# Masking the diagonal block of the first score pass with one 128-row product instead of two 64-row products

## The chip, the cores and the metric

The kernel runs on one core of one Trainium2 chip. The time is the device time of that core in microseconds (us), as a median of several runs; lower is better. A core has a matrix engine (TensorE, here PE) that multiplies a loaded block of weights (up to 128 rows by 128 columns) with a stream of columns and writes to PSUM, and VectorE (DVE), ScalarE (ACT) and GpSimd (POOL) for everything else. SyncE (SP) issues DMA transfers. The engines run side by side and wait for one another on semaphores. PE's records are of two kinds: PEld is the load of weights, PE the product. Their ends are modelled from the size of the product, so start-to-start steps say more than durations.

## The reference

Two layers run one after the other on x of shape (2, 512, 128), conditioned by one row of 128 per batch. The first is a gated recurrent layer and an MLP with ternary weights and quantised activations. The second is causal attention with 16 heads of 8 columns and an MLP. The change touches only the scores of that attention:

```python
qkv = (x @ Wqkv).reshape(b, t, 3, H, hd).transpose(2, 0, 3, 1, 4)
q, k, v = (qkv[0], qkv[1], qkv[2])
scores = jnp.einsum('bhqd,bhkd->bhqk', q, k) * hd ** (-0.5)
causal = jnp.tril(jnp.ones((t, t), bool))
scores = jnp.where(causal, scores, -jnp.inf)
attn = jax.nn.softmax(scores, axis=-1)
out = jnp.einsum('bhqk,bhkd->bhqd', attn, v)
```

## The kernel before

The first layer takes the first half of the time, up to about 140 us. Then queries and keys are computed in fp32 and split into three bf16 parts each; DMAs stack six pairs of parts (8 rows each, 48 rows in all) into the tiles `QS` and `KS`, so that one bf16 product with 48 contracted rows gives a score at nearly fp32 accuracy. Heads 0 to 7 lie in rows 0 to 63 of these tiles and heads 8 to 15 in rows 64 to 127: a product uses one half of the array's rows, the lower or the upper one (`half_rows`).

Attention runs over eight groups (two batches, four groups of four heads: two heads of each half). A group goes through two passes:

- First pass: for each tile of 128 queries the scores are computed with queries on PSUM's partitions (`score_item`, L1401 to L1403), and VectorE takes their row maxima (L1139). There are 12 items in a group (`S_ITEMS`). Items 0 to 3 have two heads each, for query tiles 0 (128 keys) and 1 (256 keys). Items 4 to 7 have one head each for query tile 2 (384 keys), and items 8 to 11 for query tile 3 (512 keys), with heads of the two halves in turn. Three PSUM banks hold items in rotation, so an item waits until the item three places earlier has been read. After the last item VectorE splits the maxima into three bf16 parts (L1149 to L1152), PE transposes them (L1413), VectorE copies them (L1160), and a DMA puts them as three more rows into `QS`.
- Second pass: the scores again, transposed and less their maxima, in `exp_slot` (L1437 with masks L1440 and L1443, always for a head of each half together). ScalarE takes the exponential (L707), PE multiplies by the values (L1457) and transposes the result (L1290), and VectorE divides (L1168, L1169).

The two passes of different groups are interleaved by an order that is written out by hand in the code: a loop of rounds, in which PE takes score item i of group n, and after certain items a slot of the second pass of group n-1 or n-2 (`E_OLD`, `E_NEW`), the values of group n-2 (`PV_AT`) or the transposes of group n-3. So after items 2, 3, 5, 6 and 10 whole-array work follows (L1413, L1290, L1457), and after the other items a half-array product. VectorE takes the items in the same order. PE's queue is in program order.

The mask of the diagonal block is added on PE. Of each score product the last 128 key columns are the block with the query tile's own tokens. A matrix of -1e30 above the diagonal is added to it by products of an identity with the mask, accumulated into the same PSUM columns as the scores. As each head uses only 64 rows of the array, there are two such products: the first 64 query rows (`pickLo` with `maskQlo`, 128 columns) and the last 64 (`pickHi` with `maskQhi`, 64 columns, since the first 64 keys are allowed to all of them). The constants lie in `k_b` (bf16), a cast (L856) of `k_f`, which one DMA loads (L336).

Of the kernel before, what the change touches and what calls it, by code (L numbers as in the profile page):

```python
# [31 lines left out]
P = 128  # L32
# [18 lines left out]
def _spans(*items):  # L51
    at, out = 0, {}
    for name, width in items:
        out[name] = (at, at + width)
        at += width
    return out, at
# [7 lines left out]
                  ("ba4", OUT6), ("bproj", D), ("b2", D))  # L64
CC, CC_N = _spans(("cT", B), ("g", 2), ("be", 2), ("b1", 4), ("bada", 4))
R1, R1_N = _spans(("bgate", 2 * D))
KC, KC_N = _spans(("ident", P), ("pickLo", P), ("pickHi", P), ("maskQlo", P), ("maskQhi", P // 2),
                  ("maskKlo", P // 2), ("maskKhi", P), ("count", 16))

W4_ROUND = (0, 1, 2, 5)  # L70
# [10 lines left out]
SROWS = HD * len(Q_PART)  # L81
# [55 lines left out]
def build(nc, x, cond_w, wa4, cond_rows, main_w, l1_w, bcast_rows, cols, rows1, consts, out):  # L137
    with ExitStack() as ctx:
# [5 lines left out]
        def bank(i, n=1):  # L144
            return ps[:, i * 512:(i + n) * 512]
# [112 lines left out]
        ident = k_f[:, slice(*KC["ident"])]  # L258
        ident_b = k_b[:, slice(*KC["ident"])]

        def k_of(name, rows):
            return k_b[rows, slice(*KC[name])]

        def half_rows(j, n=ROWS):

            first = j // 2 * ROWS
            return slice(first, first + n)

        def slot_head(g, j):
            return g * 2 + j % 2  # L270

        def tok(t, n=D):

            return slice(t * n, (t + 1) * n)
# [18 lines left out]
        def cs_of(k, i, j=1):  # L293


            return cs[:, k, i:i + j]
# [4 lines left out]
        def weights(name, c=None):  # L301

            a, z = (CW if name in CW else MW)[name]
            n = {"wa2": D, "wm2": D}.get(name, z - a)
            return (cwq if name in CW else mwq)[:, a + (c or 0) * n:a + (c or 0) * n + n]
# [901 lines left out]
        def _(pe):  # L1207
            T = nc.tensor
# [44 lines left out]
            for i, j in enumerate((0, 1, 3, 4)):  # L1253
                ins = T.matmul(bank(4)[:, 16 + B * i:16 + B * (i + 1)], lw[:, a + j * D:a + (j + 1) * D], scT[:, :],
                               start=True, stop=True)
# [6 lines left out]
            for b in range(B):  # L1262
                ins = T.matmul(bank(4)[:, b:b + 1], crow[:, a + b * P:a + (b + 1) * P], cs_of(4, 7),
                               start=True, stop=True)
# [4 lines left out]
            for b in range(B):  # L1269
                for a in range(0, OUT6, 512):  # L1270
                    z = min(a + 512, OUT6)
                    for c in range(OC):
                        ins = T.matmul(bank(2 * b + a // 512)[:, 0:z - a], cxq[:, c, b:b + 1].to_broadcast([P, P]),
                                       w4q[:, c, a:z], start=(c == 0), stop=(c == OC - 1))
# [4 lines left out]
            for i, j in enumerate((2, 5)):  # L1279
                for b in range(B):  # L1280
                    dst = bank(5)[:, (2 * i + b) * D:(2 * i + b + 1) * D]
                    T.matmul(dst, scT[:, b:b + 1].to_broadcast([P, P]), lw[:, a + j * D:a + (j + 1) * D],
                             start=True, stop=False)
                    ins = T.matmul(dst, ones[0:1, :], row1[:, g0 + i * D:g0 + (i + 1) * D], start=False, stop=True)
# [44 lines left out]
            for t in range(NT):  # L1329
                for b in range(B):  # L1330
# [5 lines left out]
                    for j in range(2):  # L1336
                        ins = T.matmul(bank(4 * b + 2 * (t % 2) + j), xq3[b][:, 1, tok(t)],
                                       weights("wm1")[:, j * MLP:(j + 1) * MLP], start=True, stop=True)
# [31 lines left out]
            for b in range(B):  # L1370
# [3 lines left out]
                for i in range(2):  # L1374
                    T.matmul(bank(4 * b + 2 + i), lw[:, a + i * D:a + (i + 1) * D], xmT[b][:, :],
                             start=True, stop=True).then_inc(S["qk_pe"], 1)
                for t in range(NT):
                    ins = T.matmul(bank(4 * b)[:, tok(t)], xmT[b][:, tok(t)], lw[:, a + 2 * D:a + 3 * D],
                                   start=True, stop=True)
                ins.then_inc(S["v_pe"], 1)  # L1380

            def score_item(n, i):

                b, g = divmod(n, NG)
                k = NUMBER[n, i]
                qt, h0, nh = S_ITEMS[i]
                w = (qt + 1) * P
                if k >= 3:
                    pe.wait_ge(S["s_used"], k - 2)
                if i == 0:  # L1390
                    pe.wait_ge(q_stacked[b], 32 * len(Q_PART))
                    pe.wait_ge(k_stacked[b], K_SP)
                    pe.wait_ge(k_stacked_gp[b], K_GP)
                    pe.wait_ge(S["part2"], 2 * B)
                    pe.wait_ge(S["v_ready"], B)
                    pe.wait_ge(S["v_ones"], b + 1)
                for j in range(nh):
                    h = slot_head(g, h0 + j)
                    dst = bank(S_BANKS[k % 3])[:, j * w:(j + 1) * w]
                    rows, r = half_rows(h0, SROWS), half_rows(h0)  # L1400
                    T.matmul(dst, QS[b][rows, h, tok(qt)], KS[b][rows, h, 0:w], start=True, stop=False)  # L1401
                    T.matmul(dst[:, w - P:w], k_of("pickLo", r), k_of("maskQlo", r), start=False, stop=False)  # L1402
                    ins = T.matmul(dst[:, w - P // 2:w], k_of("pickHi", r), k_of("maskQhi", r), start=False, stop=True)  # L1403
                ins.then_inc(S["s_pe"], 1)

            def maxima(n):
# [83 lines left out]
            def down(b, t, c, dst):  # L1490

                pe.wait_ge(S["gelu_ready"], 4 * b + c + 1)
                return T.matmul(dst, hid[b][:, c * L + t * P:c * L + (t + 1) * P], w2_g[:, b, c * D:(c + 1) * D],  # L1493
                                start=(c == 0), stop=(c == MLP // P - 1))
# [3 lines left out]
            for n in range(N_GROUPS + 3):  # L1498
                for i in range(len(S_ITEMS)):
                    if n < N_GROUPS:  # L1500
                        score_item(n, i)
                    if i == 2 and 1 <= n <= N_GROUPS:
                        maxima(n - 1)
                    if i in E_OLD and 2 <= n <= N_GROUPS + 1:
                        exp_slot(n - 2, E_OLD[i])
                    if i in E_NEW and 1 <= n <= N_GROUPS:
                        exp_slot(n - 1, E_NEW[i])
                    if i == 3 and n >= 3:
                        values_rows(n - 3)
                    if i in PV_AT and 2 <= n <= N_GROUPS + 1:  # L1510
                        values(n - 2, PV_AT[i])
                    if n == N_GROUPS and i == 7:
                        pe.wait_ge(S["s_used"], NUMBER[N_GROUPS - 1, "maxima"] + 1)
                        columns_of_attention(0)
                if n == N_GROUPS:
                    projection(0)
                if n == N_GROUPS + 1:
                    norm_columns(0)
# [6 lines left out]
            for t in range(NT):  # L1525
                for c in range(MLP // P):
                    ins = down(0, t, c, bank(W2_BANKS[0])[:, tok(t)])
# [3 lines left out]
            for c in range(MLP // P):  # L1531
                for t in range(NT):
                    ins = down(1, t, c, bank(W2_BANKS[1] + t)[:, 0:D])
# [66 lines left out]
```

## Time and profile before

| | |
|---|---|
| median of the runs | 289.58 us (289.57 to 290.57, 3 runs) |
| the profiled execution's own time | 289.72 us |
| its span, first to last instruction | 287.6 us |
| PE busy | 160.0 us, 56% |
| VectorE busy | 188.6 us, 66% |
| ScalarE busy | 139.1 us, 48% |
| L1401, 128 products | 36.5 us |
| L1402, 128 products | 27.2 us |
| L1403, 128 products | 23.9 us |
| mean granted clock | 0.798 |

Times inside the profile count from the first instruction. A busy time is the time in which at least one record of the engine or line is open. PE's records overlap, and each goes on for some time after its last column has entered, so PE's busy time is no sum of work. The granted clock is the share of TensorE's full clock that the chip grants: 1.00 is 2.4 GHz, 0.50 is 1.2 GHz. Idle time in brackets names what ended it.

### The profile page before, as it was taken

How to read it: one execution, taken by the hardware profiler on the slowest of the kernel's cores; microseconds unless marked ns; L12 is line 12 of the kernel's file. 1: busy time of each engine (PE TensorE's matmuls, PEld its weight loads, DVE VectorE, ACT ScalarE, POOL GpSimd, SP SyncE). 2: the span in 40 equal slices, each digit the busy share in tenths (PEclk: the TensorE clock that was granted, in tenths of full speed). 3: DMA queues.
4: the chain of work that ended last, by engine and by line, in shares of the span. 5: the costliest groups of instructions: out<-in, count | busy, mean ns of one | idle time of the engine just before them, and what ended most of it. 6: DMA issues, size and time to landing. Idle time of an engine off the chain costs nothing.

```text
span 287.6 us, 4182 instructions
## 1 busy us (share of the span) xinstructions
PE 160.0 (56%) x1493; PEld 102.1 (35%) x1495; DVE 188.6 (66%) x528; ACT 139.1 (48%) x297; POOL 69.5 (24%) x77
## 2 busy tenths in 40 slices
PE   0212239444733006227580009579999999897985
PEld 0102135243512003027350006254564456354664
DVE  0687797999966985965852009657897788715320
ACT  3455877557845036933164000045466446676621
POOL 7061621326035152960168000000000000003110
PEclk9999999857555556857777555559999999999999
DMA  6992000000000000000048555500000000000010
GB/s 190 417 396 125 1 0 0 0 2 1 0 0 1 0 0 0 1 2 0 0 72 89 69 69 72 70 4 4 4 3 1 5 4 2 4 2 3 0 39 36
DMA packets 5355, 12.15 MB, mean 42 GB/s; under 512 B 1075, under 2 KB 3604, under 8 KB 4692
## 3 DMA queue, kind: packets, MB, share of 16 engines
q1 hardware_dynamic: 4758, 11.09, 14.8%
q0 software_dynamic: 576, 0.79, 2.1%
q8 instruction: 12, 0.20, 0.3%
q14 instruction: 9, 0.07, 0.1%
HBM read 8.11 MB, written 0.52 MB: 30 GB/s over the span
## 4 chain that ended last, share of the span: by engine, by line
DVE 37%; PE 33%; DMA 10%; POOL 5%; SPq 5%; ACT 4%; issue 4%; DVEq 0%; ACTq 0%
DVE negmax L1139 9%; PE ps L1457 6%; DMA KS<-part 6%; PE ps L1290 5%; SPq L326 4%; PE ps L1401 4%; POOL uh L445 3%; DMA QS<-nmT 3%; PE ps L1487 2%; PE ps L1493 2%; DMA cw<-in_cond_w 2%; PE ps L1349 2%; PE ps L1437 2%; DVE xhat L810 2%; DVE u L967 2%
## 5 line engine op out<-in xcount | busy, mean ns | idle before, releaser
L1139 DVE TENSOR_REDUCE negmax<-ps 128x1 f32<-128x384 f32 (+3 forms) x96 | 52.6, 594 | 35.7 <-PE ps L1403 35.7
L707 ACT ACTIVATE PT<-ps 128x1024 f32<-128x1024 f32 x40 | 40.7, 1026 | 63.8 <-PE ps L1443 63.6
L1401 PE MATMUL ps<-KS,QS 48*128 48x384 bf16 (+3 forms) x128 | 36.5, 344 | 21.1 <-DMA KS<-part 20.8
L379 POOL TENSOR_TENSOR rstd<-veps,mhalf 128x4 f32<-128x4 f32 x8 | 8.1, 1016 | 139.9 <-DVE veps L804 139.9
L1290 PE MATMUL ps<-k_f,u 128*128 128x128 f32 x40 | 10.0, 426 | 34.4 <-ACT u L631 23.4
L1437 PE MATMUL ps<-QS,KS 51*128 51x512 bf16 (+3 forms) x128 | 24.6, 315 | 5.1 <-DMA QS<-nmT 5.0
L1402 PE MATMUL ps<-k_b 64*128 64x128 bf16 x128 | 27.2, 245 | 0.0
L1401 PEld LDWEIGHTS ps<-KS,QS 48*128 48x128 bf16 x128 | 11.7, 100 | 37.5 <-issue 22.5
L1403 PE MATMUL ps<-k_b 64*128 64x64 bf16 x128 | 23.9, 208 | 0.0
L1457 PE MATMUL ps<-PT,V 128*9 128x512 f32 (+3 forms) x256 | 22.5, 434 | 1.9 <-ACT PT L707 1.2
L1290 PEld LDWEIGHTS ps<-k_f,u 128*128 128x128 f32 x40 | 7.6, 221 | 36.2 <-DVE u L967 28.1
L1443 PE MATMUL ps<-k_b 64*128 64x128 bf16 x128 | 18.2, 222 | 0.0
L1440 PE MATMUL ps<-k_b 64*128 64x64 bf16 x128 | 17.5, 196 | 0.0
L1403 PEld LDWEIGHTS ps<-k_b 64*128 64x128 bf16 x128 | 13.2, 111 | 6.7 <-issue 2.4
L379 POOL TENSOR_TENSOR rms<-vms,mhalf 128x4 f32<-128x4 f32 x10 | 10.2, 1033 | 21.0 <-DVE vms L941 20.8
L1220 PE MATMUL ps<-k_f,cq 2*128 2x2 f32 x14 | 2.3, 249 | 19.0 <-DVE cq L830 19.0
L810 DVE TENSOR_SCALAR xhat<-xs,bnmv,rstd 128x128 f32<-128x128 f32 x32 | 10.8, 401 | 3.0 <-POOL rstd L379 2.9
L1402 PEld LDWEIGHTS ps<-k_b 64*128 64x128 bf16 x128 | 12.2, 104 | 0.0
L1437 PEld LDWEIGHTS ps<-QS,KS 51*128 51x128 bf16 x128 | 9.4, 96 | 7.1 <-DMA QS<-nmT 6.0
L1349 PE MATMUL ps<-k_f,uh 128*128 128x128 f32 x32 | 6.4, 386 | 9.7 <-DVE uh L1102 9.7
L445 POOL TENSOR_TENSOR uh<-prod,brow 128x512 f32<-128x512 f32 x8 | 9.8, 1270 | 5.2 <-DVE prod L1089 5.2
L1443 PEld LDWEIGHTS ps<-k_b 64*128 64x128 bf16 x128 | 9.2, 98 | 3.0 <-issue 0.6
(200 smaller groups left out, 435.0 us busy)
## 6 DMA issues: line engine op xcount, KB each, us to landing
w<-in_wa SPq DMA_DIRECT2D x2, 1152.0 KB, 10.7
QS<-part SPq DMA_DIRECT2D x24, 64.0 KB
brow<-in_bcast_rows SPq DMA_DIRECT2D x1, 1152.0 KB, 15.9
lw<-in_l_w SPq DMA_DIRECT2D x1, 1152.0 KB
mw<-in_main_w SPq DMA_DIRECT2D x1, 1024.0 KB, 13.5
KS<-part POOLq DMA_DIRECT2D x12, 64.0 KB, 5.6
KS<-part SPq DMA_DIRECT2D x12, 64.0 KB
cw<-in_cond_w SPq DMA_DIRECT2D x1, 576.0 KB, 5.9
```

The source lines that it names most:

```text
L379: return nc.gpsimd.tensor_tensor(r, v, mhalf[0:v.shape[0], 0:v.shape[-1]], ALU.pow)
L445: nc.gpsimd.tensor_tensor(uh[b][:, t, :], prod[b][t % 2][:, :], brow_of("nm2"), ALU.mult).then_inc(S["uh_raw"], 1)
L707: nc.scalar.activation(PT[n % 2][:, s, :], bank(2 * (use % 2), 2), ACT.Exp).then_inc(S["p_ready"], 1)
L1139: V.tensor_reduce(negmax[n % 2][:, qt, h0:h0 + nh], bank(S_BANKS[k % 3])[:, 0:nh * w].rearrange("p (h w) -> p h w", w=w), AX.X, ALU.max, n ...
L1290: ins = T.transpose(dst[:, tok(t)], src(t), ident)
L1401: T.matmul(dst, QS[b][rows, h, tok(qt)], KS[b][rows, h, 0:w], start=True, stop=False)
L1402: T.matmul(dst[:, w - P:w], k_of("pickLo", r), k_of("maskQlo", r), start=False, stop=False)
L1403: ins = T.matmul(dst[:, w - P // 2:w], k_of("pickHi", r), k_of("maskQhi", r), start=False, stop=True)
L1437: T.matmul(dsts[half], KS[b][rows, h, tok(kt)], QS[b][rows, h, kt * P:L], start=True, stop=False)
L1440: T.matmul(dsts[half][:, 0:P // 2], k_of("pickLo", r), k_of("maskKlo", r), start=False, stop=False)
L1443: ins = T.matmul(dsts[half][:, 0:P], k_of("pickHi", r), k_of("maskKhi", r), start=False, stop=True)
L1457: ins = T.matmul(bank(6)[32 * j:32 * j + HD + 1, kt * P:L], V1[b][:, kt, g * HG + j, :], src, start=(kt == 0), stop=(kt == 2))
```

## The change

Each score product gets one mask product instead of two. It takes the whole 128 by 128 identity as weights and the whole 128 by 128 mask as stream, over all 128 rows of the array, whichever half the head lies in. The constants lose two of their blocks (192 columns become 128). The second pass keeps its two masks.

```diff
-KC, KC_N = _spans(("ident", P), ("pickLo", P), ("pickHi", P), ("maskQlo", P), ("maskQhi", P // 2),
+KC, KC_N = _spans(("ident", P), ("pickLo", P), ("pickHi", P), ("maskQ", P),
                    ("maskKlo", P // 2), ("maskKhi", P), ("count", 16))
...
-                    rows, r = half_rows(h0, SROWS), half_rows(h0)
+                    rows = half_rows(h0, SROWS)
                     T.matmul(dst, QS[b][rows, h, tok(qt)], KS[b][rows, h, 0:w], start=True, stop=False)
-                    T.matmul(dst[:, w - P:w], k_of("pickLo", r), k_of("maskQlo", r), start=False, stop=False)
-                    ins = T.matmul(dst[:, w - P // 2:w], k_of("pickHi", r), k_of("maskQhi", r), start=False, stop=True)
+                    ins = T.matmul(dst[:, w - P:w], ident_b, k_of("maskQ", slice(0, P)), start=False, stop=True)
...
-        "consts": _np.concatenate([eye, eye[lo], eye[hi], mask_q[lo], mask_q[hi][:, P // 2:], mask_k[lo][:, :P // 2],
+        "consts": _np.concatenate([eye, eye[lo], eye[hi], mask_q, mask_k[lo][:, :P // 2],
```

On PE this is the place around items 8 and 9 of a round. A row is the line, the operation, what it writes and reads, and the shape of its output; L1457 is the values, L1401 the score product, L1402 and L1403 its masks, L1437 to L1443 a slot of the second pass. Before:

```order
L1457 MATMUL ps<-PT,V 9x128 x4
L1401 MATMUL ps<-KS,QS 128x512
L1402 MATMUL ps<-k_b 128x128
L1403 MATMUL ps<-k_b 128x64
L1401 MATMUL ps<-KS,QS 128x512
L1402 MATMUL ps<-k_b 128x128
L1403 MATMUL ps<-k_b 128x64
L1437 MATMUL ps<-QS,KS 128x512 x2
```

After, at the same place (lines behind L1402 have moved up by one):

```order
L1456 MATMUL ps<-PT,V 9x128 x4
L1401 MATMUL ps<-KS,QS 128x512
L1402 MATMUL ps<-k_b 128x128
L1401 MATMUL ps<-KS,QS 128x512
L1402 MATMUL ps<-k_b 128x128
L1436 MATMUL ps<-QS,KS 128x512 x2
```

One row of each score product is gone, 128 in all, and nothing has changed its place; L1402 now reads all 128 rows. On VectorE only the cast at L856 has another width (720 instead of 784 columns), on SyncE only the load of the constants.

## Rows read from the trace of the kernel before

**Rows 1.** The page, busy time of the engines over the whole span

```profile
PE 160.0 (56%) x1493; PEld 102.1 (35%) x1495; DVE 188.6 (66%) x528; ACT 139.1 (48%) x297; POOL 69.5 (24%) x77
```

**Rows 2.** Stretches: busy us (count) of PE, PEld, DVE, ACT, POOL, PEclk, DMA share, GB/s

```profile
172.18:181.50 9.32, 9.01 (x75) 5.76 (x77) 8.46 (x20) 0.00 (x0) 0.00 (x0) 0.50 0.58 72
...
187.00:188.00 1.00, 0.00 (x0) 0.00 (x0) 0.00 (x0) 0.00 (x0) 0.00 (x0) 0.50 0.13 17
188.85:194.86 6.01, 5.96 (x71) 4.25 (x72) 4.43 (x11) 4.07 (x4) 0.00 (x0) 0.50 0.01 1
...
199.59:248.28 48.69, 45.21 (x682) 25.28 (x680) 39.33 (x96) 27.38 (x31) 0.00 (x0) 1.00 0.01 3
```

**Rows 3.** Timeline of VectorE: start us, us, operation, count, [idle before <-releaser]

```profile
216.90 0.56 DVE L1139 TENSOR_REDUCE negmax<-ps 128x1 f32<-128x384 f32 x1 [0.65 <-PE ps L1403]
...
219.06 0.69 DVE L1139 TENSOR_REDUCE negmax<-ps 128x1 f32<-128x512 f32 x1 [0.49 <-PE ps L1403]
```

**Rows 4.** Timeline of PE, the stretch that PE leads

```profile
215.47 1.04 PE L1457 MATMUL ps<-PT,V 128*9 128x512 f32 x8
216.45 0.33 PE L1401 MATMUL ps<-KS,QS 48*128 48x384 bf16 x1
216.62 0.22 PE L1402 MATMUL ps<-k_b 64*128 64x128 bf16 x1
216.68 0.19 PE L1403 MATMUL ps<-k_b 64*128 64x64 bf16 x1
216.80 0.83 PE L1457 MATMUL ps<-PT,V 128*9 128x384 f32 x8
217.56 0.33 PE L1401 MATMUL ps<-KS,QS 48*128 48x384 bf16 x1
217.57 0.39 PE L1437 MATMUL ps<-QS,KS 51*128 51x512 bf16 x1
```

**Rows 5.** Timeline of PE around the transposes of L1413 and L1290

```profile
213.04 0.39 PE L1413 MATMUL ps<-k_b,nmpart 128*12 128x128 bf16 x4 [0.61 <-DVE negmax L1139]
213.37 0.28 PE L1401 MATMUL ps<-KS,QS 48*128 48x256 bf16 x1
...
213.75 0.19 PE L1403 MATMUL ps<-k_b 64*128 64x64 bf16 x1
213.87 0.66 PE L1290 MATMUL ps<-k_f,pvs 128*128 128x128 f32 x4
214.46 0.33 PE L1401 MATMUL ps<-KS,QS 48*128 48x384 bf16 x1
```

**Rows 6.** Timeline of PE, whole-array and one-row products in one accumulation

```profile
50.38 0.48 PE L1284 MATMUL ps<-row,ones 1*128 1x128 f32 x2
50.79 0.49 PE L1282 MATMUL ps<-lw,scT 128*128 128x128 f32 x2
```

**Rows 7.** Timeline of PE's weight loads at the place of rows 4

```profile
216.46 0.10 PEld L1402 LDWEIGHTS ps<-k_b 64*128 64x128 bf16 x1
...
216.79 0.12 PEld L1457 LDWEIGHTS ps<-PT,V 128*9 128x9 f32 x8
```

**Rows 8.** Timeline of PE at the lower clock, up to the restart

```profile
180.54 0.59 PE L1413 MATMUL ps<-k_b,nmpart 128*12 128x128 bf16 x4 [0.25 <-DVE negmax L1139]
181.06 0.39 PE L1401 MATMUL ps<-KS,QS 48*128 48x256 bf16 x1
...
188.90 0.61 PE L1437 MATMUL ps<-QS,KS 51*128 51x512 bf16 x2 [5.01 <-DMA QS<-nmT]
```

**Rows 9.** Timeline of PE at score items 8 and 9

```profile
218.56 0.40 PE L1401 MATMUL ps<-KS,QS 48*128 48x512 bf16 x2
...
218.87 0.39 PE L1437 MATMUL ps<-QS,KS 51*128 51x512 bf16 x2
...
219.18 0.38 PE L1401 MATMUL ps<-KS,QS 48*128 48x512 bf16 x1
```

**Rows 10.** Timeline of VectorE, the first wait after the cast of the constants

```profile
10.40 0.16 DVE L766 TENSOR_TENSOR wraw<-ps,k_f 128x2 f32<-128x2 f32 x1 [1.72 <-PE ps L1214]
```

## The prediction

> **What bounds the kernel now.** First the page: no engine is full over the span, PE 56%, VectorE (DVE) 66%, ScalarE (ACT) 48% [rows 1]. The change touches only the attention stage, so these shares decide nothing. Next the table by stretches [rows 2]: the 48.69 us from 199.59 to 248.28 are five equal rounds of 9.74 us at a granted clock of 1.00, each with the 12 score items of one group of four heads. Divided by five, a PE record is open for 9.04 us of a round (records overlap, so PE's work is less), VectorE works for 7.87 us and ScalarE for 5.48. Who waits for whom tells more. In the round that ends at 219.06, VectorE [rows 3] waits for PE ahead of three of the larger items, the first time 0.65 us up to 216.90, the last time 0.49 us up to 219.06. PE waits for VectorE too, 0.61 us before the transposes of L1413 [rows 5]. The round is a chain that changes sides: PE leads from 215.47 [rows 4] to 219.06, some 3.6 us, VectorE most of the rest. Neither has much room.
>
> **What is removed and added.** Per score product (16 in a round, 128 in all) L1402 and L1403 go. L1403 starts 0.06 us after L1402 (216.62, 216.68 [rows 4]) and streams 64 columns, half of that, 0.03 us: together 0.09 us. The new product has 128 rows and 128 columns in bf16. The nearest row is L1413 [rows 5]: four records open for 0.39 us, one of them 0.22 (L1402's length, the same 128 columns), so a step of 0.17 / 3 = 0.056 us. By steps alone the change saves 0.03 us a product, 0.5 us a round.
>
> **The price that the diff doesn't show.** L1401 uses 48 rows of one half of the array, the new product all 128. Before, PE passes between half-array and whole-array work six times each way in a round. Read what a passage costs:
> - half to whole: L1403 starts at 216.68, its stream ends at 216.71, L1457 starts at 216.80: 0.09 us [rows 4]. The same from 213.75 to 213.87 ahead of L1290 [rows 5].
> - whole to half: the last L1413 starts at 213.21, streams to 213.26, and L1401 starts at 213.37: 0.10 us [rows 5].
> - in one accumulation: L1282 (128 rows) and L1284 (1 row) alternate in pairs into the same tile [rows 6], 0.41 us from pair to pair. Records of L1290, of the same 128 fp32 columns, take (214.46 - 213.87 - 0.10) / 4 = 0.12 us each [rows 5]; a pair so carries 0.17 us beyond two of them.
> - the weight load of a first product after a passage starts with the product, not ahead of it: L1457's at 216.79, while L1402's, within one half, starts 0.16 us before its product [rows 4, 7].
>
> So each mask costs 0.09 in, 0.056 for itself and 0.10 out, 0.25 us instead of 0.09. Eleven of 16 are enclosed by half-array work and pay both ways. Five (after items 2, 3, 5, 6 and 10) are followed by whole-array work and add only the way in before themselves; the one behind was paid before.
>
> No row shows this passage with bf16 on both sides and 128 weight columns. The bounds are 0 (the product joins like one more of the half's) and 0.14 us (at the lower clock: the last L1413 starts at 180.82, streams 0.11 us, L1401 starts at 181.06 [rows 8]). I take 0.09 and 0.10, since every passage that I read, fp32 or bf16, with 9, 12 or 128 weight columns, has about that.
>
> The Trainium skill, TensorEngine Tiling (Array Packing), Key Properties, says that a change of tiling mode drains the engine. It gives no time, and the sum doesn't use it.
>
> **What is lost beside it.** Items 8 and 9 lie in different halves and run side by side: both L1401 of 512 columns are in one 0.40 us row [rows 9]. So do L1401 and L1437 at 217.56 and 217.57 [rows 4]. A whole-array mask between them puts them one behind the other.
>
> **PE's work in one round of the changed kernel**, from start-to-start steps at full clock:
> - 16 score products, the step from L1401 to L1402 is 0.17 us for 384 columns [rows 4] and, by 0.053 per 128 columns, 0.06, 0.12 and 0.22 for 128, 256 and 512; four of each: 2.28
> - 16 masks of 0.056: 0.90
> - second pass (L1437, L1440, L1443), both halves side by side: 0.31 us for 512 columns (218.87 to 219.18 [rows 9]), so 0.09 beyond the columns' step; 0.31 + 0.26 + 0.21 + 0.15, twice: 1.86
> - values (L1457), from start to the next half-array product 0.98 for 512 columns and 0.76 for 384 [rows 4], so 0.22 per 128 columns, 0.54 and 0.32 for the other two; less four passages: 2.24
> - L1413 0.22, and L1290 0.49 (213.87 to 214.46 [rows 5], less a passage): 0.71
> - 17 passages in (16 masks, and L1457 after item 7's second pass) at 0.09, 17 out at 0.10: 3.2
>
> Together 11.2 us; a mask and an L1457 behind it are different whole-array forms, which may cost up to 0.09 three times. I take 11.3 us. That is over 9.74, so PE has no wait left and sets the time. The about 1 us that PE now waits hides the first part of the growth; VectorE's 7.87 and ScalarE's 5.48 us fit inside.
>
> **The sum.** Five rounds: 5 x (11.3 - 9.74) = +7.8. From the restart at 188.90 to 199.59 the clock is 0.50 until 194.86 [rows 2, 8]; a stream of 128 columns takes 0.107 us there and a passage about 0.13: 12 products at 0.37 instead of 0.18, 4 at +0.16, two pairs that no longer overlap, less PE's waits: +2.5 (1.6 to 4). Before that PE is already the slow side (9.01 of 9.32 us busy [rows 2]); 22 products at +0.19 move the copy of the first maxima by 4.2 us. But PE then waits 5.01 us for the DMA of these maxima [rows 8], and until about 187 the DMA engines still move what was issued earlier (from 187 to 188 they are 0.13 busy, and idle after the restart [rows 2]). So most is covered; the rest of group 1's items stays, +1.0 (0 to 2). After the last round three more items: +0.5. Behind the attention stage nothing changes. Sum +11.8 us on the profiled execution's own 289.72 us (span 287.6): 301.5. The median of the runs shown, 289.58, is 0.14 lower; I keep 301.5.
>
> The constants shrink from 784 to 720 columns. Their cast gets 64 of 784 columns shorter, and VectorE's next step waits 1.72 us for PE [rows 10]. Whatever of the cast is saved, a few hundredths of a us, is swallowed by that wait, and would be the whole gain without it.
>
> **Rivals.**
> - *The passage is free*, because the identity is loaded ahead and only both halves have to be done. Then a product saves 0.03 us, and the lost overlaps cost about as much in the 3.6 us that PE leads: 289 to 290 us, not slower. For it speaks that both operands are bf16 and that 8,192 fewer columns stream; against it the weight loads of [rows 7]. It decides below about 0.015 us a passage.
> - The Trainium skill, TensorE: Matmul & The Clock Gate, Part 2, step 1, would give this case: a weight load for the background buffer is pulled ahead of running products.
> - *Half the price*, 0.045 a way, since the whole-array product here is short: 34 x 0.05 less per round, so 9.6 to 10.4 us and 291 to 296.
> - *The clock stays down.* It is 0.50 while single halves work (172 to 181 us) and rises at 194.86, after 6 us in which both halves mostly work side by side [rows 2]. The change takes away much of that overlap. Each us by which the rise is late costs about 0.4 us. Should it not rise in the rounds, the 8.0 us of streams double: some 50 us more, about 350.
>
> **How the numbers follow.** Full price, the clock up within 7 us of its present place: 0.66, 297 to 308, likeliest 301.5. Half price 0.11, free 0.11, clock lost or much later 0.12. The range of 291 to 311 leaves out the free case and most of the lost clock. A measurement of this kernel tells about 0.5%, 1.4 us, from no change; the free case lies mostly inside that, with a third of it faster. Faster 0.04, same 0.08, slower 0.88.
>
> **What would show it.** 0.09 us between the end of L1401's stream and the mask, 0.10 between mask and next L1401; the mask's weight load starting with it; the L1401 of items 8 and 9 about 0.45 us apart; rounds of 11.3 us with PE never waiting; the wait of 5.01 us shrunk to below 2. It is wrong if the mask starts 0.01 to 0.02 us after L1401's stream: then the rounds are about 9.7 us and the time doesn't change.

## The result, and the profile after

The changed kernel is slower: ratio 1.0508 to the kernel before, interval [1.0453, 1.0563], which on 289.57 us is 304.3 us. The median of its four runs is 312.59 us, because two took 303.95 and 304.85 us at a mean granted clock of 0.797 and two 320.32 and 321.44 us at 0.743; the ratio is made from the first two, and why the others had less clock is open. The profiled execution took 303.95 us, its span 301.9 (before 289.72 and 287.6). The prediction was 301.5 us, 291 to 311.

The page of the changed kernel has, for the busy times of [rows 1] and then the chain of work that ended last:

```profile
PE 185.7 (62%) x1365; PEld 102.4 (34%) x1367; DVE 193.0 (64%) x528; ACT 139.9 (46%) x297; POOL 69.6 (23%) x77
...
PE 49%; DVE 26%; DMA 7%; POOL 5%; SPq 4%; ACT 4%; issue 3%; DVEq 0%; ACTq 0%
```

PE is busy for 25.7 us more with 128 fewer products. PE now carries 49% of the chain and VectorE 26%; before it was the other way round, 33% and 37%.

The table by stretches, with the columns of [rows 2]. The stretches are: from the first group's items to the restart with the second pass, the restart up to the clock's rise, the rest of that round, one round, five rounds:

```profile
172.00:186.60 14.60, 14.60 (x52) 5.17 (x51) 11.25 (x23) 0.00 (x0) 0.00 (x0) 0.50 0.47 62
186.60:200.50 13.90, 13.90 (x89) 5.31 (x88) 7.75 (x17) 5.12 (x5) 0.00 (x0) 0.50 0.00 1
200.50:203.60 3.10, 3.10 (x33) 1.11 (x29) 1.12 (x3) 0.73 (x1) 0.00 (x0) 1.00 0.02 5
203.60:215.30 11.70, 11.70 (x121) 5.30 (x120) 8.31 (x19) 5.62 (x7) 0.00 (x0) 1.00 0.01 2
203.60:262.11 58.51, 58.51 (x601) 26.52 (x600) 41.56 (x95) 28.04 (x31) 0.00 (x0) 1.00 0.01 2
```

The last row answers to the last one of [rows 2]: five rounds take 58.51 us instead of 48.69, so 11.70 each instead of 9.74, and PE is busy in every moment of them. Before, it was 45.21 of 48.69. VectorE has the same instructions (a record of it is open for 8.3 us a round, 7.9 before) and waits for the rest. The first row shows that the wait of 5.01 us [rows 8] is gone: PE works through.

Rounds are cut where VectorE starts the maxima of item 8 (L1139). These starts are at 176.82, 190.29, 199.59 us and then every 9.74 up to 248.28 before; after, at 177.43, 188.14, 203.60 and then every 11.70 up to 262.11. The span's +14.35 us so falls apart into four pieces:

| piece | before | after | difference |
|---|---|---|---|
| start to item 8 of group 1 | 190.29 | 188.14 | -2.15 |
| item 8 of group 1 to item 8 of group 2 | 9.30 | 15.46 | +6.16 |
| five rounds | 48.69 | 58.51 | +9.82 |
| item 8 of the last group to the end | 39.29 | 39.81 | +0.52 |

The timeline of PE in the changed kernel, at the place that answers to [rows 4 and 9] (L1456 is now the values, L1436 the second pass):

```profile
222.91 0.23 PE L1402 MATMUL ps<-k_b 128*128 128x128 bf16 x1
223.07 1.05 PE L1456 MATMUL ps<-PT,V 128*9 128x512 f32 x8
...
226.41 0.39 PE L1401 MATMUL ps<-KS,QS 48*128 48x512 bf16 x1
226.73 0.23 PE L1402 MATMUL ps<-k_b 128*128 128x128 bf16 x1
226.90 0.39 PE L1401 MATMUL ps<-KS,QS 48*128 48x512 bf16 x1
227.22 0.23 PE L1402 MATMUL ps<-k_b 128*128 128x128 bf16 x1
227.38 0.39 PE L1436 MATMUL ps<-QS,KS 51*128 51x512 bf16 x2
```

From L1401 to its mask it is 0.32 us. Four times 0.053 of that is the stream of 512 columns, 0.11 the passage into whole-array work. From the mask to the next L1401 it is 0.17, 0.056 stream and 0.11 the way out. Items 8 and 9, which were one row of two before [rows 9], now start 0.49 us apart. The weight loads at the same place:

```profile
226.41 0.09 PEld L1401 LDWEIGHTS ps<-KS,QS 48*128 48x128 bf16 x1 [0.22 <-DVE negmax L1139]
226.73 0.10 PEld L1402 LDWEIGHTS ps<-k_b 128*128 128x128 bf16 x1 [0.23 <-issue]
226.89 0.09 PEld L1401 LDWEIGHTS ps<-KS,QS 48*128 48x128 bf16 x1
```

The mask's weights load at 226.73, with their product and 0.32 us after the load before. The load's queue was idle for the 0.23 us ahead of it, and the profile puts this idle time down to nothing that it shows ("issue").

VectorE's side is seen in its timeline at items 6 and 8, which answer to the two rows of [rows 3] (0.65 and 0.49 us of waiting there), and in the waits of the five rounds (engine, line, waited for: us in total, times, longest):

```profile
224.59 0.56 DVE L1139 TENSOR_REDUCE negmax<-ps 128x1 f32<-128x384 f32 x1 [0.84 <-PE ps L1402]
...
227.00 0.69 DVE L1139 TENSOR_REDUCE negmax<-ps 128x1 f32<-128x512 f32 x1 [0.67 <-PE ps L1402]
```

```profile
ACT PT L707 <- PE ps L1442: 33.8, 26, 3.4
DVE negmax L1139 <- PE ps L1402: 15.5, 25, 0.8
```

The same view of the kernel before (199.59 to 248.28 us) has 23.3 us and 9.0 us there, and a wait of PE for VectorE that the changed kernel no longer has:

```profile
ACT PT L707 <- PE ps L1443: 23.3, 16, 2.0
DVE negmax L1139 <- PE ps L1403: 9.0, 16, 0.7
PE ps L1413 <- DVE negmax L1139: 3.0, 5, 0.6
```

### The profile page after: what moved, and what is told of

Read it like the earlier page. It is cut to its first block, busy times and chain, and to the rows that moved or that the text cites. A ratio compares the mean times of both kernels' runs of the same rounds, so it can differ in the third digit from the quotient of the medians.

```text
span 301.9 us, 3926 instructions
## 1 busy us (share of the span) xinstructions
PE 185.7 (62%) x1365; PEld 102.4 (34%) x1367; DVE 193.0 (64%) x528; ACT 139.9 (46%) x297; POOL 69.6 (23%) x77
## 4 chain that ended last, share of the span: by engine, by line
PE 49%; DVE 26%; DMA 7%; POOL 5%; SPq 4%; ACT 4%; issue 3%; DVEq 0%; ACTq 0%
PE ps L1401 11%; PE ps L1402 8%; PE ps L1456 7%; DMA KS<-part 5%; PE ps L1290 4%; PE ps L1436 4%; SPq L326 4%; POOL uh L445 3%; PE ps L1486 2%; PE ps L1492 2%; DMA cw<-in_cond_w 2%; PE ps L1349 2%; DVE xhat L810 2%; DVE u L967 2%; PE ps L1442 1%
## 5 line engine op out<-in xcount | busy, mean ns | idle before, releaser
L1139 DVE TENSOR_REDUCE negmax<-ps 128x1 f32<-128x384 f32 (+3 forms) x96 | 56.4, 600 | 46.8 <-PE ps L1402 45.3
L1401 PE MATMUL ps<-KS,QS 48*128 48x128 bf16 (+3 forms) x128 | 44.6, 348 | 19.6 <-DMA KS<-part 19.6
L1402 PE MATMUL ps<-k_b 128*128 128x128 bf16 x128 | 31.8, 249 | 0.0
L1290 PE MATMUL ps<-k_f,u 128*128 128x128 f32 x40 | 10.0, 426 | 34.6 <-ACT u L631 23.4
L1401 PEld LDWEIGHTS ps<-KS,QS 48*128 48x128 bf16 x128 | 12.4, 97 | 41.3 <-issue 22.7
L1456 PE MATMUL ps<-PT,V 128*9 128x512 f32 (+3 forms) x256 | 23.3, 447 | 1.5 <-ACT PT L707 1.2
L1402 PEld LDWEIGHTS ps<-k_b 128*128 128x128 bf16 x128 | 12.6, 98 | 25.1 <-issue 20.4
L1290 PEld LDWEIGHTS ps<-k_f,u 128*128 128x128 f32 x40 | 7.6, 220 | 36.4 <-DVE u L967 28.1
L1436 PE MATMUL ps<-QS,KS 51*128 51x512 bf16 (+3 forms) x128 | 19.0, 321 | 0.0
L1442 PE MATMUL ps<-k_b 64*128 64x128 bf16 x128 | 13.3, 223 | 0.0
L1439 PE MATMUL ps<-k_b 64*128 64x64 bf16 x128 | 12.2, 199 | 0.0
L586 ACT ACTIVATE junk<-mx 128x128 f32<-128x128 f32 x16 | 4.7, 297 | 11.3 <-DVE mx L936 11.3
L1349 PEld LDWEIGHTS ps<-k_f,uh 128*128 128x128 f32 x32 | 5.8, 206 | 10.0 <-DVE uh L1102 10.0
L1492 PEld LDWEIGHTS ps<-w_g,PT 128*128 128x128 f32 x64 | 7.8, 191 | 2.6 <-issue 1.4
```

The lines of the kernel that those rows point to most:

```text
L1139: V.tensor_reduce(negmax[n % 2][:, qt, h0:h0 + nh], bank(S_BANKS[k % 3])[:, 0:nh * w].rearrange("p (h w) -> p h w", w=w), AX.X, ALU.max, n ...
L1290: ins = T.transpose(dst[:, tok(t)], src(t), ident)
L1349: ins = T.transpose(bank(4 * b + c)[:, tok(t)], uh[b][:, t, tok(c)], ident)
L1402: ins = T.matmul(dst[:, w - P:w], ident_b, k_of("maskQ", slice(0, P)), start=False, stop=True)
L1436: T.matmul(dsts[half], KS[b][rows, h, tok(kt)], QS[b][rows, h, kt * P:L], start=True, stop=False)
L1442: ins = T.matmul(dsts[half][:, 0:P], k_of("pickHi", r), k_of("maskKhi", r), start=False, stop=True)
```

## The experiments

The kernel before had medians of 288.48 to 288.83 us on the chips of these runs. The length of a round is that of the rounds at full clock; "first round" is the one from item 8 of group 1 to item 8 of group 2, in which the clock rises. A visit is a stay in whole-array work, with a passage in and a passage out.

### The mask as two whole-array products

```diff
-ins = T.matmul(dst[:, w - P:w], ident_b, k_of("maskQ", slice(0, P)), start=False, stop=True)
+mask = k_of("maskQ", slice(0, P))
+T.matmul(dst[:, w - P:w - P // 2], ident_b, mask[:, 0:P // 2], start=False, stop=False)
+ins = T.matmul(dst[:, w - P // 2:w], ident_b, mask[:, P // 2:P], start=False, stop=True)
```

> The changed kernel, but each whole-array mask product is issued as two of 64 columns, one right behind the other. Passages between half-array and whole-array work: 17 each way in a round as before. If the price is that of the passage (measured in the changed kernel: 0.10 us in, 0.105 out), the second product only adds what a 64-column step costs more than its columns, 0 to 0.03 us: rounds of 11.7 to 12.2 us against 11.70, 304 to 308 us. If every whole-array product costs about 0.25 us because of its size or its weights, wherever it stands, the round grows by 16 x 0.25 = 4 us and the kernel takes about 335 us.

Ratio 1.0627 [1.0524, 1.0730]; the interval overlaps that of the changed kernel, so the totals don't tell the two apart and the rounds have to. A round takes 11.77 us, 0.07 more than with one product and not the 4 us more of the rival. The timeline of PE in this kernel:

```profile
215.45 0.39 PE L1401 MATMUL ps<-KS,QS 48*128 48x512 bf16 x1
215.77 0.20 PE L1403 MATMUL ps<-k_b 128*128 128x64 bf16 x1
215.81 0.19 PE L1404 MATMUL ps<-k_b 128*128 128x64 bf16 x1
215.94 0.39 PE L1438 MATMUL ps<-QS,KS 51*128 51x512 bf16 x2
```

The second half of the mask starts 0.04 us after the first; only the way in (0.32 from L1401, as before) and the way out (0.13, 0.10 beyond a stream of 0.03) carry the price. It belongs to the change of form, not to the product.

### One mask for two heads

Items 0 to 3 take both scores first and then one product of 256 mask columns (the mask read twice) for both. The edit, cut down to the products themselves:

```diff
-T.matmul(dst, QS[b][rows, h, tok(qt)], KS[b][rows, h, 0:w], start=True, stop=False)
-ins = T.matmul(dst[:, w - P:w], ident_b, k_of("maskQ", slice(0, P)), start=False, stop=True)
+T.matmul(dst, QS[b][rows, h, tok(qt)], KS[b][rows, h, 0:w], start=j == 0, stop=False)
+# behind the loop over the item's heads:
+T.matmul(bank(...)[:, 0:nh * w].rearrange("p (h w) -> p h w", w=w)[:, :, w - P:w], ident_b,
+         k_of("maskQ", slice(0, P)).unsqueeze(1).to_broadcast([P, nh, P]), start=False, stop=True)
```

> The changed kernel, but items 0 to 3, which have two heads in one bank, take both score products first and then one mask product over both diagonal blocks (256 columns, the mask read twice). The columns streamed are the same; passages fall from 17 to 13 each way. Passage theory: 4 x 0.2 us less in a round, 10.9 instead of 11.70 us, and about 1 us less in each of the two groups at the lower clock: 297 to 299 us. If the columns or rows of the mask set the price: no change, 304 us.

Ratio 1.0395 [1.0299, 1.0491], round 10.85 us: 0.85 less than 11.70 for four visits to whole-array work and back fewer, so 0.21 us each.

### The same, and items 8 and 9 with both scores ahead of both masks

```diff
-if n < N_GROUPS:
+if n < N_GROUPS and i == 8:
+    score_item(n, 8, (0,))
+    score_item(n, 9, (0,))
+    score_item(n, 8, (1,))
+    score_item(n, 9, (1,))
+elif n < N_GROUPS and i != 9:
     score_item(n, i)
```

`(0,)` calls for the scores of an item alone and `(1,)` for its mask.

> As the kernel with paired masks, and in addition items 8 and 9 issue both score products (one in each half, so side by side) and then both masks: 12 passages each way, and the overlap of these two comes back. Passage theory with lost overlap: 0.2 us for the passage and about 0.25 us for the overlap less, rounds of about 10.4 us, 293 to 296 us. If overlap is worth nothing: 10.7 us and 296 to 298. If neither counts: as the kernel with paired masks.

Ratio 1.0295 [1.0194, 1.0395], round 10.43 us. The timeline of PE has items 8 and 9 together again, and both masks in one row:

```profile
211.01 0.39 PE L1401 MATMUL ps<-KS,QS 48*128 48x512 bf16 x2
211.33 0.28 PE L1403 MATMUL ps<-k_b 128*128 128x128 bf16 x2
211.55 0.39 PE L1438 MATMUL ps<-QS,KS 51*128 51x512 bf16 x2
```

What started in 0.97 us before the second pass (226.41 to 227.38 of the changed kernel) starts in 0.54. The difference of 0.43 is that of the rounds, 10.85 to 10.43. It is one stream of 512 columns (0.21) and two passages (0.21). With five of the sixteen visits for a mask gone, the kernel is still 3% slower than before.

### The masks' columns alone: the kernel before without its second mask

This kernel leaves L1403 out, so that the last 64 queries of each diagonal block are unmasked in the first pass.

```diff
-T.matmul(dst[:, w - P:w], k_of("pickLo", r), k_of("maskQlo", r), start=False, stop=False)
-ins = T.matmul(dst[:, w - P // 2:w], k_of("pickHi", r), k_of("maskQhi", r), start=False, stop=True)
+ins = T.matmul(dst[:, w - P:w], k_of("pickLo", r), k_of("maskQlo", r), start=False, stop=True)
```

> The kernel before with its second mask product (L1403) left out: the last 64 rows of each diagonal block stay unmasked. One mask product instead of two, as in the change, but without a passage. If the product itself is worth what its step says (0.03 us on three or four products in the part of a round that PE leads), 288.5 to 289.6 us. If fewer products in the first pass free VectorE-led parts too, below 288. If it takes more than 290, the loss of the changed kernel has a cause beside the passages.

Ratio 1.0027 [0.9950, 1.0104], no difference beyond the noise; round 9.65 instead of 9.74. (Its first round took 10.59 us, with the clock low up to 196.8 us.) This is all that one mask product less could bring if it cost no passage: 0.09 us a round for 16 products whose work is 0.03 us each. The rest of their 0.5 us has to lie where PE would wait anyway.

### Meant to take the overlap alone away: the heads of one half behind one another

The kernel before, with the heads of items 4 to 11 in the order 0, 1, 2, 3 instead of 0, 2, 1, 3, so that items 8 and 9 use the same half.

```diff
-... for j in (0, 2, 1, 3)]
+... for j in (0, 1, 2, 3)]
```

> The kernel before with another order of heads: items 4 to 7 and 8 to 11 take the heads of the lower half first and then those of the upper, instead of in turn, so items 8 and 9 lie in the same half and can't run side by side. No mask is changed and no passage added. This is the lost overlap by itself. By the trace of before the pair is worth about 0.3 us in the part of a round that PE leads: rounds of 9.9 to 10.0 us instead of 9.74 and 290.5 to 292 us. If VectorE's pace hides it: 289 to 290.

Ratio 1.0045 [0.9997, 1.0094]: at most a small loss. The table by stretches, the first round and the five behind it:

```profile
188.90:200.14 11.24, 11.24 (x126) 6.26 (x124) 7.72 (x17) 5.20 (x6) 0.00 (x0) 0.62 0.01 3
200.14:248.83 48.69, 45.66 (x682) 25.81 (x680) 39.34 (x95) 27.53 (x31) 0.00 (x0) 1.00 0.01 3
```

The rounds at full clock are what they were, 9.74 us; the expectation for them was missed. The timeline of PE shows why:

```profile
219.42 0.38 PE L1401 MATMUL ps<-KS,QS 48*128 48x512 bf16 x1
219.43 0.39 PE L1437 MATMUL ps<-QS,KS 51*128 51x512 bf16 x1
219.64 0.22 PE L1402 MATMUL ps<-k_b 64*128 64x128 bf16 x1
```

The overlap is not lost but moved: item 9 now starts together with the second pass behind it, so from item 8 to the values behind item 10 it is 1.06 instead of 1.01 us. So this run doesn't show what an overlap is worth. Only the first round, mostly at half the clock, is longer, 11.24 instead of 9.30 us; its clock rose at 197.5 us, 2.4 us later than in the kernel before, so the order of heads need not be the reason.

### The clock raised ahead, in the changed kernel and in the kernel before

88 independent products of 384 columns ahead of the first score item and 30 (in the kernel before 36) ahead of the first slot of the second pass, into a bank that is free then.

```diff
+def fill(count):
+    for _ in range(count):
+        T.matmul(bank(6)[:, 0:3 * P], ident_b, k_b[:, 0:3 * P], start=True, stop=True)
```

> The changed kernel with filling products (whole-array, 384 columns, into a bank that is free) while PE waits for the stacked keys before the first score item (88 of them) and 30 more before the first second-pass slot. Theory that the late rise of the granted clock costs the rest of the loss and makes the time differ from run to run: the clock is 1.00 from the first score item on, the round from item 8 of group 1 to that of group 2 falls from 15.5 to about 11.5 us, 297 to 301 us, with runs close together. If the clock falls back between, or if the stretch is bound by something else: no change, 304, or more by what the filling delays.

> The kernel before with the same filling (88 products before the first score item, 36 in the 5 us wait for the first maxima's DMA). Before, the clock rises 6 us after the restart. If that costs as much as in the changed kernel, about 0.4 us for each us at the lower clock: 2 us less, 286 to 288. If the round at the lower clock (9.3 us) is bound by VectorE: no change, 288.5 to 290.

The changed kernel with it: ratio 1.0726 [1.0686, 1.0766], slower than without. The table by stretches, before and behind the clock's first fall, and the five rounds:

```profile
170.50:175.07 4.57, 4.57 (x25) 2.26 (x25) 3.31 (x7) 0.00 (x0) 0.00 (x0) 1.00 0.57 75
175.07:188.73 13.66, 13.66 (x48) 5.32 (x48) 8.75 (x19) 0.00 (x0) 0.00 (x0) 0.50 0.30 41
...
207.39:265.90 58.51, 58.51 (x601) 26.52 (x600) 41.57 (x96) 28.06 (x31) 0.00 (x0) 1.00 0.01 2
```

The clock was at 1.00 when the score items began, and fell at 175.07 though PE never waited. It was up again at 188.73, but fell once more at 195.55 and came back only at 205.79. The second block of filling was too long as well: it held PE up to 191.76, while the first exponential stands at 187.5 without it. So this run does not tell what an early clock would be worth: of its expectation the other branch came, the clock fell back and the filling delayed the rest. It does show that in this kernel a high clock at the start did not last, and that a round at full clock is 11.70 us with or without.

The kernel before with it: ratio 1.0118 [1.0082, 1.0154], so slower by 1.2%, and its median of 290.92 us lies above both expected ranges. Here too the second filling was too long: PE came to the second pass at 189.57 us, 18.5 us after the first maxima instead of 16.0. The clock fell at 175.31, rose at 185.55 and stayed. The first round then lies wholly at full clock:

```profile
190.38:199.48 9.10, 8.15 (x126) 4.56 (x124) 7.42 (x18) 5.38 (x6) 0.00 (x0) 1.00 0.02 4
```

It takes 9.10 us instead of 9.30. In the kernel before, 4.8 us of low clock so cost 0.2 us: at full clock PE has gaps in this round (8.15 of 9.10 us busy), and at the low clock it uses them up (9.30 of 9.30).

### Fewer passages in the kernel before: the values in two pairs

The kernel before with its own masks. The values, four blocks of eight L1457, come in pairs after items 5 and 10 instead of one by one after items 5, 6, 7 and 10.

```diff
-PV_AT = {5: 0, 6: 1, 7: 3, 10: 2}
+PV_AT = {5: (0, 1), 10: (3, 2)}
...
-    values(n - 2, PV_AT[i])
+    for kt in PV_AT[i]:
+        values(n - 2, kt)
```

> The kernel before with two passages less in a round and nothing else: the four blocks of values (L1457) are issued as two pairs, after items 5 and 10, instead of one after each of items 5, 6, 7 and 10. Same products, same columns. Passage theory: 0.19 us for each pair of passages in the part of the round that PE leads, rounds of 9.35 to 9.5 us instead of 9.74, 287 to 288.5 us. If passages cost nothing here, or VectorE leads that part once PE is faster: no change, 289.5; if the later items 6 and 7 starve VectorE: 290 to 292.

Ratio 0.9924 [0.9882, 0.9965], median 285.0 us: faster by 0.8%, and more than was expected. A round takes 9.19 us. The timeline of PE:

```profile
212.95 1.69 PE L1457 MATMUL ps<-PT,V 128*9 128x512 f32 x16
214.57 0.34 PE L1401 MATMUL ps<-KS,QS 48*128 48x384 bf16 x2
```

Sixteen products of the values in one visit, and behind them items 6 and 7 side by side, which the values had kept apart [rows 4]. At 0.2 us each, two visits fewer are 0.4 us of the 0.55, in the stretch that PE leads; the rest may be the two items side by side, which no run tells apart.

### That, and the transposes of L1290 moved next to those of L1413

```diff
+if i == 2 and n >= 3:
+    values_rows(n - 3)
...
-if i == 3 and n >= 3:
-    values_rows(n - 3)
```

> As the kernel with the values in two pairs, and the transposes of L1290 moved from behind item 3 to right behind the transposes of L1413 (item 2), so that one more pair of passages goes. This one lies in the part of a round that VectorE leads. If a passage is only worth something where PE leads: rounds of 9.2 us as before or up to 0.3 us longer, because item 3 now comes 0.3 us later: 285 to 287 us. If each pair of passages is worth 0.19 us wherever it is: 9.0 us and 284.

Ratio 0.9951 [0.9912, 0.9990], round 9.60 us, 0.4 more than without the move and more than either branch had expected. The timelines of PE and VectorE:

```profile
208.93 0.39 PE L1413 MATMUL ps<-k_b,nmpart 128*12 128x128 bf16 x4 [0.61 <-DVE negmax L1139]
209.25 0.65 PE L1290 MATMUL ps<-k_f,pvs 128*128 128x128 f32 x4
209.84 0.28 PE L1401 MATMUL ps<-KS,QS 48*128 48x256 bf16 x1
...
210.44 0.69 DVE L1139 TENSOR_REDUCE negmax<-ps 128x2 f32<-128x512 f32 x1 [0.32 <-PE ps L1403]
```

One passage more is saved, but item 3 comes 0.6 us later to VectorE, which sets the pace at this place (PE waits 0.61 us for it at L1413), and VectorE now waits 0.32 us for it. The delay outweighs the passage. What the passage would be worth here without a delay isn't shown.

### One mask for two heads, 8 and 9 together, and the values in pairs

The third experiment with the edit of `PV_AT` above.

> The kernel with whole-array masks, paired over items 0 to 3 and over items 8 and 9 (rounds of 10.43 us), and the values in two pairs after items 5 and 10. There the order of masks and values matters otherwise: items 6 and 7 now stand between half-array work and pay a way out that the values took over before, so the two passages saved by pairing the values come back at items 6 and 7. Passage theory: 12 passages each way as before, PE sets the pace, so no gain: rounds of 10.3 to 10.5 us, 295 to 297 us. If grouping the values is worth 0.5 us in a round by itself, as in the kernel with half-array masks (9.74 to 9.20): 9.9 us and 292.

Ratio 1.0143 [1.0081, 1.0204], round 10.09 us, 0.34 less than 10.43. The expectation of next to nothing was missed: it took a block of values behind a mask to share the mask's visit for free. The timeline of PE shows that it doesn't:

```profile
215.88 0.28 PE L1403 MATMUL ps<-k_b 128*128 128x256 bf16 x1
216.00 0.60 PE L1290 MATMUL ps<-k_f,pvs 128*128 128x128 f32 x4
...
217.62 0.23 PE L1403 MATMUL ps<-k_b 128*128 128x128 bf16 x1
217.78 1.69 PE L1458 MATMUL ps<-PT,V 128*9 128x512 f32 x16
```

From 256 mask columns to L1290, which also loads 128 weight columns, it is 0.12 us, little more than the stream of 0.107. From 128 mask columns to the values, which load 9 weight columns, it is 0.16, 0.10 beyond the stream. So the pairs save one passage after item 6 and two after item 7, 0.3 us.

## Why the prediction was right

Direction and size came out (+11.8 us forecast on the profiled execution, +14.2 measured, the median's ratio gives +14.7). Step by step:

**The price of a passage: right.** 0.09 and 0.10 were read from other forms; over the 16 masks of a round (215.19 to 226.90 us) the steps from L1401 to L1402 sum to 3.78 us, 2.13 of it streams, so 0.103 a way in. The steps from mask to half-array work are 0.162 us, 0.106 beyond the stream. The rival of a free passage falls with that (it wanted the mask 0.01 to 0.02 us behind the stream), the rival of half the price too. That the price is per change of form, not per product, was argued from rows and is shown by the split mask (0.07 us a round more instead of the 4 us that a price per product would have given).

**The weight load starts with the mask's product: right.** It was at 226.73 us, 0.32 us after the load before. The Trainium skill, TensorE: Matmul & The Clock Gate, Part 2, step 1, says that a load for the background buffer is pulled ahead of running products; between these forms it wasn't. The Trainium skill, TensorEngine Tiling (Array Packing), Key Properties, says that a change of tiling mode drains the engine, and the runs agree that such a change costs time, 0.10 us. How much of the 0.10 us is a drain and how much is a weight load that is no longer hidden, no run separates.

**PE never waits, rounds of 11.3 us: the mechanism right, one term too small.** The rounds are 11.70. The same sums, over the round above: L1401 to its mask 3.78 (forecast 3.72), mask to half-array work 1.78 (1.72), second pass 1.94 (1.95), values 2.63 (2.64, of which the forecast took the ways out off at 0.09 and put them back at 0.10, 0.04 us too much), L1412 and L1290 0.86 (0.91), and mask to whole-array work, five times, 0.70 (0.28 and the 0.1 allowed). The term that failed is the last, "a mask and an L1457 behind it are different whole-array forms, which may cost up to 0.09 three times": it is due in full, at 0.10, at the three blocks of values, and before the transposes of L1412 too, where 12 weight columns follow 128. So 9 or 12 weight columns act as another form than 128. The timeline of PE in the changed kernel has both kinds:

```profile
220.15 0.23 PE L1402 MATMUL ps<-k_b 128*128 128x128 bf16 x1
220.31 0.39 PE L1412 MATMUL ps<-k_b,nmpart 128*12 128x128 bf16 x4
...
221.22 0.23 PE L1402 MATMUL ps<-k_b 128*128 128x128 bf16 x1
221.28 0.61 PE L1290 MATMUL ps<-k_f,pvs 128*128 128x128 f32 x4
```

0.16 us from the mask to 12 weight columns, 0.06, its stream alone, to 128. The other way round it is the same: in the kernel with the transposes moved together, L1290 starts 0.32 us after L1413, 0.22 of it streams. Four times 0.10 instead of the 0.1 taken makes 0.3 of the missing 0.4 us, and passages of 0.105 instead of 0.09 and 0.10 most of the rest. Over five rounds that is 2.0 us, +9.8 instead of +7.8. Two experiments bear out the price: 4 visits fewer are 0.85 us, 3 passages fewer 0.34.

**The lost overlap: right in the changed kernel, where it stands in the sum.** Items 8 and 9 were to start about 0.45 us apart, and start 0.49 apart. With them together the round is 0.43 shorter, half of it the overlap. What the loss would be worth in the kernel before stays open, since the run meant for it only moved the overlap.

**From the restart to the round of group 2: too small, +6.2 instead of +2.5.** The first round, before and after:

```profile
190.29:199.59 9.30, 9.30 (x126) 5.71 (x124) 7.60 (x18) 5.21 (x6) 0.00 (x0) 0.74 0.01 4
188.14:203.60 15.46, 15.46 (x109) 5.88 (x108) 8.21 (x18) 5.21 (x6) 0.00 (x0) 0.60 0.01 2
```

It has less to do than a later one: the block of values behind item 10 (0.55 us in the changed kernel, 216.46 to 217.01) and L1290 (0.44) aren't due yet, 109 records instead of 121. At full clock it would so take about 11.70 - 0.99 = 10.71 us in the changed kernel, an estimate from these steps; before it takes 9.10 (the kernel before with filling). That is 1.6 of the 6.16 us. The rest is the low clock. In the changed kernel it lasts 12.36 us of the round (188.14 to 200.50) and costs 15.46 - 10.71 = 4.75 us, 0.38 us per us; the same estimate gives 0.38 to 0.42 for the other five kernels with the whole-array mask. Before, 4.8 us of it cost 0.2 us. (It isn't cheap there for long: in the kernel without its second mask product 8.2 us of it went with a first round of 10.59 us.)

Two terms of the step were too small. The clock was taken to rise about where it did; it rose at 200.50 instead of 195.04, which at 0.38 is 2.1 us of the missing 3.7. The other 1.6 lie in "less PE's waits": PE's longer work was to be hidden in part by waits of PE, but in the kernel before the low clock had already used them up (9.30 of 9.30 us busy), so the growth came through in full. The timeline of PE at the low clock:

```profile
187.25 0.63 PE L1401 MATMUL ps<-KS,QS 48*128 48x512 bf16 x1
187.81 0.29 PE L1402 MATMUL ps<-k_b 128*128 128x128 bf16 x1
188.03 0.60 PE L1401 MATMUL ps<-KS,QS 48*128 48x512 bf16 x1
```

0.56 us is 0.427 of stream and 0.13 of passage, 0.22 is 0.107 and 0.11: the passages were priced right there.

**The start: -2.15 instead of +1.0.** The cover by the DMA was read right and held fully. From the first maxima to item 8 of group 1 it was 17.38 us and is 17.15: the copy of the first group's maxima comes 3.8 us later behind the first maxima (4.2 were forecast), and the wait from it to the first exponential shrinks from 8.38 to 4.33 us. The other 1.9 us are the first maxima themselves, at 170.99 instead of 172.91, and arise ahead of any mask: the first score product starts at 170.03 instead of 172.18. The other kernels with the whole-array mask have them from 170.77 to 171.17, those with the masks of before from 170.08 to 172.13. So other executions with the masks of before lie on both sides of 170.99; whether the shorter constants have a part in it is not shown.

**The clock's rival.** "Each us by which the rise is late costs about 0.4 us" was right, 0.38. The clock did rise in every profile taken. But with the whole-array mask it rose late each time: 12.6 to 14.3 us after PE's start on the second pass, in the five such kernels without filling, against 3.9 to 10.0 us in the five with the masks of before. Each is one profile. Why it rises later behind whole-array masks is not settled: it was tried to raise it ahead, and it fell again during the first group's items in both kernels.

**The tail and the casts:** +0.52 (0.5 forecast); nothing was seen of the shorter constants.

The two misses in the middle (+2.0 and +3.7) and the start (-3.15) sum to the 2.55 us between +11.8 and the span's +14.35. That the total came out so close is in part luck: the rounds and the low clock were both priced too low, and had the start come out as forecast, the span would have grown by 14.35 + 3.15 = 17.5 us.

## What to carry to other kernels

Count what PE changes between, not what it streams: a product of another form (half or whole array, other width of weights) in the midst of others cost two passages of 0.10 us here, against the 0.03 us that it saved. Group the products of one form where PE leads, which gave 0.8% here, but not at the price of making an engine wait that sets the pace: moving the transposes together lost 0.4 us a round. A low clock of 4.8 us cost only 0.2 us while PE had gaps to give, and 0.38 us per us once the change had filled them.

## What the runs showed of the hardware

- Between two whole-array products, a change from 128 to 9 or 12 weight columns costs 0.10 us, as much as a change between half and whole array; from 12 to 128 it is the same (209.25 us in the kernel with the transposes moved). A change of type from bf16 to fp32 with 128 weight columns in both costs nothing (0.06 us for a stream of 0.056).
- The granted clock can fall with PE never idle: in the changed kernel with filling it fell from 1.00 at 175.07 us, and PE's records were open for 4.57 of the 4.57 us before. In the kernel before with filling it fell at 175.31, with 4.18 of 4.81 us busy. In the changed kernel it stayed at 0.50 from 172.00 to 200.50 with PE's records open in every moment.
- Products of different halves start out of program order: in the kernel with the heads in the order 0, 1, 2, 3 the second pass's L1437 starts 0.01 us behind item 9's L1401, ahead of item 9's own masks, which come before it in the program. It is so in the kernel before, too: L1437 at 217.57 us, item 7's own mask only at 217.73.
